# A selective-scan and mixture-of-experts kernel: a new lead-in, and the steady order of the rounds from the first round on

## What is computed

```python
xr = x @ W_in;  xi, res = jnp.split(xr, 2, axis=-1)
u = silu(conv4(xi) + conv_b)
dbc = u @ W_x                       # 8 columns for delta, 16 for B, 16 for C
delta = softplus(dbc[..., :8] @ W_dt + b_dt)
h = exp(delta * A) * h + delta * B * u        # a scan over time, 16 states
y = (sum_n h * C + u * D) * silu(res)
x = x + y @ W_out
scores = norm(x) @ gate_w.T;  cw = softmax of the two best, else 0
x = x + sum_e cw[e] * (silu(norm(x) @ w1[e].T) @ w2[e].T)
```

## Time and profile before

| | us |
|---|---|
| median of 3 runs | 1105.02 |
| lowest and highest | 1104.96, 1106.01 |
| profiled execution, its own time | 1103.15 |
| span of its trace, first to last instruction | 1101.2 |

### The profile page before, as it was taken

How to read it: one execution, slowest core, us unless ns; L and a number is a source line. 1 busy time by engine, 2 the same in 40 slices (tenths; PEclk the granted TensorE clock), 3 DMA queues, 4 the chain that set the end, 5 groups by cost and what they waited for, 6 DMA issues and landing times.

```text
span 1101.2 us, 18699 instructions
## 1 busy us (share of the span) xinstructions
PE 1037.8 (94%) x6152; PEld 759.1 (69%) x6152; DVE 1012.7 (92%) x1038; ACT 908.2 (82%) x1382; POOL 960.5 (87%) x892
## 2 busy tenths in 40 slices
PE   7558679999999999999999999999999999989997
PEld 4336457777777777767777777777777776767775
DVE  2799999999999999999999999999999999999721
ACT  4967578988999899899989999899989989875533
POOL 3388698998999999999999999999999999799834
PEclk9798889999999999999999999999999999989999
DMA  5321313104031311303131220403130120320000
GB/s 152 157 86 49 116 58 116 59 28 155 2 126 58 126 59 68 115 0 138 44 125 57 91 91 7 172 2 125 57 135 39 68 105 0 136 87 10 11 10 10
DMA packets 39760, 84.03 MB, mean 76 GB/s; under 512 B 5744, under 2 KB 30624, under 8 KB 31392
## 3 DMA queue, kind: packets, MB, share of 16 engines
q1 hardware_dynamic: 36848, 83.05, 21.0%
q10 hardware_dynamic: 2864, 0.38, 0.2%
HBM read 78.70 MB, written 4.72 MB: 76 GB/s over the span
## 4 chain that ended last, share of the span: by engine, by line
PE 84%; DVE 6%; ACT 4%; issue 3%; POOL 1%; DMA 0%; POOLq 0%; ACTq 0%; DVEq 0%
PE work L1384 19%; PE work L1374 18%; PE y_ps L1326 17%; PE work L1246 9%; PE rows L1305 4%; DVE h L984 4%; PE work L1265 3%; PE work L1347 3%; PE work L1230 2%; PE rows L1384 2%; PE work L1256 2%; PE rows L1374 1%; DVE rows L974 1%; PE work L1293 1%; ACT dA L742 1%
## 5 line engine op out<-in xcount | busy, mean ns | idle before, releaser
L471 POOL TENSOR_TENSOR h<-h,c_rows 128x1024 f32<-128x1024 f32 x256 | 600.4, 2367 | 75.1 <-DVE h L984 75.0
L984 DVE TENSOR_TENSOR_SCAN h<-dA,rows 128x1024 f32<-128x1024 f32 x256 | 579.4, 2276 | 1.9 <-ACT dA L742 0.7
L742 ACT ACTIVATE dA<-delta,a_neg 128x510 f32<-128x510 f32 x512 | 325.4, 708 | 1.7 <-POOL delta L455 0.5
L974 DVE TENSOR_TENSOR rows<-du,rows 128x1024 f32<-128x1024 f32 x256 | 307.1, 1213 | 3.7 <-PE rows L1305 3.6
L1326 PEld LDWEIGHTS y_ps<-ident,h 128*128 128x128 f32 x2048 | 242.6, 145 | 52.2 <-issue 36.3
L1326 PE MATMUL y_ps<-ident,h 128*128 128x128 f32 x2048 | 267.5, 278 | 2.6 <-POOL h L471 2.6
L1384 PEld LDWEIGHTS work<-w,hid 128*128 128x128 f32 x1856 | 223.2, 193 | 36.5 <-ACT hid L776 20.8
L1374 PE MATMUL work<-x2T,w 128*128 128x512 f32 x474 | 238.3, 597 | 0.3
L1384 PE MATMUL work<-w,hid 128*128 128x128 f32 x1856 | 229.0, 277 | 3.5 <-ACT hid L776 3.2
L776 ACT ACTIVATE hid<-work 128x512 f32<-128x512 f32 x237 | 139.2, 596 | 58.7 <-PE work L1374 56.8
L511 POOL TENSOR_TENSOR x<-x,weighted 128x512 f32<-128x512 f32 x128 | 163.4, 1277 | 23.4 <-DVE weighted L1053 23.0
(11 more groups left out here) (118 smaller groups left out, 953.9 us busy)
## 6 DMA issues: line engine op xcount, KB each, us to landing
c_rows<-c_dram SPq DMA_DIRECT2D x64, 1024.0 KB, 5.2
x_in<-in_x SPq DMA_DIRECT2D x16, 256.0 KB, 2.9
x_again<-in_x SPq DMA_DIRECT2D x16, 256.0 KB, 3.2
out<-x SPq DMA_DIRECT2D x16, 256.0 KB, 2.6
w<-in_w1T SPq DMA_DIRECT2D x1, 1024.0 KB, 6.3
w<-in_w2T SPq DMA_DIRECT2D x1, 1024.0 KB, 8.4
h<-in_conv_w SPq DMA_DIRECT2D x1, 512.0 KB, 4.9
c_dram<-bcd SPq DMA_DIRECT2D x16, 32.0 KB, 1.6
```

The lines of the kernel that those rows point to most:

```text
L471: nc.gpsimd.tensor_tensor(at, at, c_rows[:, n, :].unsqueeze(1).broadcast_to([P, H, T]), ALU.mult).then_inc(c_used, 1)
L742: last = nc.scalar.activation(two_seqs(dA[:, n % RING, half, :])[:, :, 1:], two_seqs(delta[:, half, :])[:, :, 1:], ACT.Exp, scale=a_neg[:, ...
L974: nc.vector.tensor_tensor(rows[:, n % 2], du[:, j.odd], rows[:, n % 2, H - 1, :].unsqueeze(1).broadcast_to([P, H, T]), ALU.mult).then_inc( ...
L984: nc.vector.tensor_tensor_scan(h[:, n % RING].rearrange("p h t -> p (h t)"), dA[:, n % RING].rearrange("p h t -> p (h t)"), rows[:, n % 2] ...
```

## The change

The lead-in is written anew in all engines, and round 0 no longer has its gate, skip and first `row_b` in it: these run where `round_` has them, in round 1.

- W_x comes in one DMA to a spare part of `h`; GpSimd copies it to its places in seven instructions. W_dt comes once more, as float32 rows `w_dt_first`, before x of round 1, which now precedes the six loads of W_dt.
- ScalarE loads Silu's table at the start by a small activation.
- VectorE makes mean and variance with `bn_aggr`; GpSimd only does the power; VectorE makes the shift. Half of the normalized x is made by ScalarE and half by VectorE. Half of `w_conv` is made by VectorE and half by GpSimd.
- WARM is 27 and not 40.
- The projection to delta, B and C starts with its first half when the first half of u is there. One ScalarE copy takes all 112 rows from the bank, and the first delta is projected from it in float32, beside the split into parts, not behind it.
- Abs and Exp run by halves on ScalarE, Relu is on VectorE, and Ln, delta and du run by halves.

```diff
+LEAD_BCD = 2
+LEAD_DT = (4, 5)
-        LOADS = 14
+        LOADS = 4
+        COPIES = 3 * H + 1
-        WARM = 40
+        WARM = 27
...
+        def weigh_taps(engine, half):
+            at = slice(half * P, (half + 1) * P)
+            engine.tensor_tensor(w_conv[:, :, at], w_in[:, at].unsqueeze(1).broadcast_to([P, TAPS, P]),
+                                 taps_rows.rearrange("p (d k) -> p k d", k=TAPS)[:, :, at],
+                                 ALU.mult).then_inc(w_conv_ready, 1)
 SyncE
                 load(skip_w[:, :], D)
+                sp.wait_ge(w_dt_first_clear, 1)
+                sp.dma_start(w_dt_first[DT_ROWS[0]:DT_ROWS[0] + RANK, :], W_dt).then_inc(w_dt_first_loaded, 16)
+                fetch_x(Round(1))
                 sp.wait_ge(dt_rows_clear, 1)
...
-                fetch_x(Round(1))
 GpSimd
             pool.wait_ge(constants_ready, CONSTANTS)
+            pool.wait_ge(w_x_loaded, 16)
+            for half in range(H):
+                part_rows = w_bc[:, half, 0:3 * SPLIT].rearrange("p (a r) -> p a r", a=3)
+                for row, src in ((0, w_x[:, half, RANK:RANK + NS]),) + tuple(
+                        (row, w_x[:, half, 0:RANK]) for row in DT_ROWS):
...
+            nc.gpsimd.tensor_copy(w_bc[:, :, C_ROW:ROWS], w_x[:, :, RANK + NS:]).then_inc(w_bc_ready, 1)
+            pool.wait_ge(variance_ready[0], 1)
+            nc.gpsimd.tensor_tensor(rstd[:, 0, :], variance[:, 0, :], power[:, 0:TB],
+                                    ALU.pow).then_inc(variance_ready[0], 1)
+            pool.wait_ge(taps_loaded, 16 * TAP_LOADS)
+            weigh_taps(nc.gpsimd, 1)
 ScalarE
             def gate_silu(j, half):
-                if not there(j) or j.led():
+                if not there(j):
             def skip(j):
-                if not there(j) or j.led():
+                if not there(j):
             def lead_in():
-                pre_norm(lead)
+                act.wait_ge(constants_ready, CONSTANTS)
+                nc.scalar.activation(warm[:, :], one[:, :], ACT.Silu).then_inc(tables_warm, 1)
+                act.wait_ge(rstd_ready[0], 1)
+                for b in range(TB // 2):
+                    last = nc.scalar.activation(xn[:, 0, b, :], x_in[:, 0, b, :], ACT.Identity,
...
                 for half in range(H):
                     conv_silu(lead, half)
-                skip(lead)
-                high(lead)
-                copy_bcd(lead)
-                middle(lead)
-                gate_silu(lead, 0)
-                low(lead)
-                gate_silu(lead, 1)
                 exp_tables()
-                for half in range(H):
-                    soft_parts(lead, half)
-                soft_exponential(lead)
-                soft_log(lead)
+                act.wait_ge(bcd_projected, 1)
+                nc.scalar.activation(bcd[0:ROWS, :], bcd_bank(lead)[0:ROWS], ACT.Copy).then_inc(bcd_ready, 1)
                 (a_neg, as before)
+                for half in range(H):
+                    act.wait_ge(dt_projected, half + 1)
+                    nc.scalar.activation(soft[:, half, :], bank(LEAD_DT[half]), ACT.Abs,
...
+                    nc.scalar.activation(soft[:, half, :], soft[:, half, :], ACT.Exp,
...
+                middle(lead)
+                for half in range(H):
+                    act.wait_ge((lead_exp, soft_exp)[half], 1)
+                    nc.scalar.activation(soft[:, half, :], soft[:, half, :], ACT.Ln,
...
+                low(lead)
 TensorE
             def project_gate(j, half, *uses):
-                if not there(j) or j.led():
+                if not there(j):
             def row_b(j, n):
-                if not there(j) or (n < 2 and j.led()):
+                if not there(j):
             def lead_in():
...
+                for half in range(H):
+                    pe.wait_ge(u_ready, half + 1)
+                    last = nc.tensor.matmul(bcd_bank(lead), w_bc[:, half, :], u[:, 0, half, :], start=(half == 0),
+                                            stop=(half == H - 1))
+                pe.wait_ge(bcd_ready, 1)
+                for half in range(H):
+                    nc.tensor.matmul(bank(LEAD_DT[half]), w_dt_first[:, half * P:(half + 1) * P], bcd[0:SPLIT, :],
+                                     start=True, stop=True).then_inc(dt_projected, 1)
                 take_high(lead)
-                project_gate(lead, 1)
                 take_middle(lead)
-                for half in range(H):
-                    delta_rank(lead, half, *([use_dt(lead, 0)] if half and DT[0] == DT[1] else []))
                 pe.wait_ge(select_ready, 1)
-                row_b(lead, 0)
-                row_b(lead, 1)
                 pe.wait_ge(dt_read, H)
```

More of the change, by code:

```diff
@@ L105, in wait, with run @@
             eng.wait_ge(sem, value)
-    def run(eng, body, stages, stop):
-        loop_first = stages + 2
+    def run(eng, body, first, stages, stop):
+        loop_first = max(first, stages + 2)
         pairs = (min(rounds, stop) - loop_first) // 2
-        for i in range(loop_first):
+        for i in range(first, loop_first):
             body(Round(i))
@@ L291, in place, with bcd_bank @@
             return k
+        def bcd_bank(j):
+            return bank(LEAD_BCD if j.lead else BCD)
         def two_seqs(ap):
@@ L424, in inverse_deviation @@
             def inverse_deviation(j, k):
-                if not there(j):
+                if not there(j) or (k == 0 and j.led()):
                     return
@@ L607, in _ @@
         def _(act):
-            def load(dst, src):
-                act.dma_start(dst, src).then_inc(weights_loaded, 16)
             act.dma_start(w_in[:, :], W_in).then_inc(taps_loaded, 16)
[L612 to L619, removed]
+            act.dma_start(w_x[:, :, :], W_x.rearrange("(h p) n -> p h n", p=P)).then_inc(w_x_loaded, 16)
             tables = ["none"]
@@ L667, in gate_silu @@
                 wait(act, gated, j.count(1, -1))
-                nc.scalar.activation(gate[:, j.odd, half, :], bank(LEAD_GATE[half] if j.lead else GATE[half]),
-                                     ACT.Silu).then_inc(gate_ready, 1)
+                nc.scalar.activation(gate[:, j.odd, half, :], bank(GATE[half]), ACT.Silu).then_inc(gate_ready, 1)
             def copy_bcd(j):
@@ L1123, in split_dt_weights, with first_norm @@
                 dve.wait_ge(dt_weights_ready, 2)
+            def first_norm():
+                pre_stats(r[0])
+                dve.wait_ge(stats_ready[0], 1)
+                for b in range(TB):
+                    last = nc.vector.bn_aggr(mean_variance[:, b, :], stats[:, 0, b, :])
+                last.then_inc(moments_ready[0], 3)
+                dve.wait_ge(moments_ready[0], 3)
+                nc.vector.tensor_scalar(variance[:, 0, :], mean_variance[:, :, 1], EPS, None,
+                                        ALU.add).then_inc(variance_ready[0], 1)
+                dve.wait_ge(taps_loaded, 16 * TAP_LOADS)
+                weigh_taps(nc.vector, 0)
+                dve.wait_ge(variance_ready[0], 2)
+                nc.vector.scalar_tensor_tensor(shift[:, 0, :], mean_variance[:, :, 0], -1.0, rstd[:, 0, :], ALU.mult,
+                                               ALU.mult).then_inc(rstd_ready[0], 1)
+                dve.wait_ge(rstd_ready[0], 1)
+                for b in range(TB // 2, TB):
+                    last = nc.vector.tensor_scalar(xn[:, 0, b, :], x_in[:, 0, b, :], rstd[:, 0, b:b + 1],
+                                                   shift[:, 0, b:b + 1], ALU.mult, ALU.add)
+                last.then_inc(lead_norm, 1)
@@ L1255, in project_gate @@
                 at = (H + half) * P
-                nc.tensor.matmul(two_seqs(bank(LEAD_GATE[half] if j.lead else GATE[half])), w_in[:, at:at + P], xnT[:, :, PAD:],
+                nc.tensor.matmul(two_seqs(bank(GATE[half])), w_in[:, at:at + P], xnT[:, :, PAD:],
                                  start=True, stop=True).then_inc(gate_projected, 1)
@@ L1264, in project_bcd @@
                 for half in range(H):
-                    last = nc.tensor.matmul(work[:, BCD, :], w_bc[:, half, :], u[:, j.odd, half, :],
+                    last = nc.tensor.matmul(bcd_bank(j), w_bc[:, half, :], u[:, j.odd, half, :],
                                             start=(half == 0), stop=(half == H - 1))
```

102 lines of the change are left out of this document (67 added, 35 removed).

## The result

The changed kernel takes 1109.56 us (median of 6 runs, 1109.33 to 1109.77) against 1105.37 us before (6 runs): a ratio of 1.0036 with a 95% interval of 1.0023 to 1.0049.

A forecast was written before the change was run, and what follows sets the result against it. The prediction took VectorE's start on its scans as the early bound, passed on to rounds where TensorE is full. Scan 2 at 45.15 and not 46.76 us gave 1105.02 less 1.6, 1103.4 us; range 1101.4 to 1105.8.

The forecast's parts named there:

- scan 2 is handed on: VectorE's scan of state 2 in round 0, at 46.76 us before: any shift is passed on one for one.
- (d): Rival: the gain is real but lost later, where TensorE takes over as the bound; 1105 us, chance 0.05.
- The sum at scan 2: Lead-in and round 1 terms added up to the start of round 0's scan 2: 45.15 us, 1.6 us earlier.
- Part 1: Lead-in until round 0's convolution starts: at 11.95 us, 1.0 us earlier, bounds 0.2 to 2.2 us.
- rival (b): TensorE's pause before the first convolution lowers its clock, costing 1.5 to 1.9 us; 1104.8 to 1105.3 us, chance 0.17.
- Part 2: Round 0's convolution to the end of ScalarE's low part: at 27.4 us; delta and du some 6 us earlier.
- Part 3: ScalarE's round 1 queue ahead of decay 0 takes the 6 us back: scan 0 at 38.2 us, 0.3 us later.
- Part 4: TensorE's round 1 convolution ends earlier, row 2 ready at 43.5 us; scan 2 hangs on VectorE alone, gaining 1.6 us.
- Rival (c): Slower: ScalarE's queue between low and decay 0 delays scan 0 by 2 to 4 us; 1105.5 to 1107.5 us, chance 0.08.

The follow-up runs named there:

- e2: The changed kernel with GpSimd's half of w_conv made by VectorE, right behind VectorE's own half: 1109.06 us.
- e4: The changed kernel with round 0's gate projections moved to the lead-in, its gate silus and skip term behind round 1's convolution silus: 1102.19 us, 0.9966 of before.
- e5: The changed kernel with nine tiny unused ScalarE activations more in the lead-in, ahead of the loop: 1108.07 us.
- e6: The changed kernel with e4's edits, w_conv's second half on VectorE behind its normalized x, 40 warm-up transposes and eleven tiny activations: 1098.38 us, 0.9942 of before.
- e1: The changed kernel with 44 warm-up transposes and not 27: 1109.44 us, 1.0029 of before.
- e3: The changed kernel with w_conv wholly on VectorE and 36 warm-up transposes and not 27: 1107.90 us.

## Why the prediction was wrong

**In short.** Three steps of the sum failed: the longer pause behind the shorter WARM, costed at nothing, took 2.8 us in the convolution of round 0; GpSimd's half of w_conv, counted as hidden, took 1.3 us in VectorE's shift; and the gate's second projection, costed at the full clock, took 1.0 us more. A stall in the loop, which no term of the sum covers, added 1.5 us.

**What bounds the kernel, and that scan 2 is handed on: right in the main.** From scan 2 of round 0 to that of round 4 the difference moves by 0.2 us at most in the changed kernel, e2, e4, e5 and e6, over differences of -5.0 to +4.2 us. It isn't one for one everywhere: in e1 and e3, and in the second trace of the kernel before, another 0.5 to 0.7 us was lost between scan 2 of round 0 and that of round 2. So the rival that a gain is lost later (d) is out for the large gains of e4 and e6, but it describes e1, where 1.0 us became 0.2.

**The sum at scan 2 was off by 5.8 us** (45.15 forecast, 50.95 measured), and its terms measure:

| term | forecast | measured |
|---|---|---|
| end of the power | 9.4 | 9.46 |
| shift | 0.2 | 1.47 |
| start of the convolution of round 0 | 11.95 | 13.56 |
| that convolution | 7.1 | 9.92 |
| end of that convolution to the end of low | 8.3 | 8.5 |
| low to scan 0 | 10.8 | 12.0 |
| scan 0 to scan 2 | 6.95 | 6.9 |

The power's end came out right by luck: W_x let the first copy begin at 6.82 and not 6.4 us and the seven copies took 0.1 us more, while the first-use cost, of which half was counted, didn't come.

Part 1 failed at the shift. I counted GpSimd's half of w_conv as hidden because nothing waits for it before 11.6 us, and didn't ask who runs beside it: VectorE's shift does, on the path, and took 1.3 us more. In e2 and e6, where GpSimd's multiply isn't beside it, the shift takes 0.16 us. The handovers between the steps are the other 0.3 us by which the convolution started later than forecast. The Trainium skill says of the shift's neighbour, in "GPSIMD Engine Reference", section Specifications: that GpSimd's interfaces to SBUF are shared with VectorE, and that they contend, among other cases, when VectorE's instruction has two inputs in SBUF. The trace agrees: the shift has two such inputs (1.47 for 0.16 us), and VectorE's multiply for w_conv, with two as well, made GpSimd's six copies 2.42 us long for 1.49. The steady rounds give no warning of it: a scan takes 2.29 us with GpSimd idle (37.92 us) and with a GpSimd multiply from 40.35 to 42.72 us beside it (41.36 us); but there one of the scan's inputs, rows, lies in PSUM.

Part 1 failed also at WARM, costed at nothing with a rival (b) of 0.17. The late shift lengthened the pause from the forecast 1.7 us to 2.86 us, and the clock fell. That this pause decides it rests on the nine traces: in the three with a pause of at most 1.81 us the convolution took 7.11 us, in the six with 2.35 us or more it took 8.57 to 10.03. The rival had the mechanism but priced it at 1.5 to 1.9 us, from the convolution of round 1, and its time ended at 1105.3 us; it was 2.8 us here. That the two faults feed each other (the later the shift, the longer the pause) is what I had not seen. The end of the 27 transposes was forecast well (9.2 us, and 9.17 measured), but again with luck: they began 0.23 us later than in the kernel before, where the first two dozen took 5.2 us and not 5.5.

Part 2 was right to 0.2 us, and the new softplus does what it should: from the end of the convolution to the end of the last Ln it is 8.1 us, where it was 12.6. VectorE's delta and du ended at 33.9 and not near 29 us, by the 4.4 us that the convolution ended late and its halves of 0.69 us for 0.62, but nothing waited for them.

Part 3 had the mechanism (what was gained is spent in ScalarE's queue ahead of decay 0) and its direction; the mis-sized term is the gate's second projection, taken at the full clock (1.05 us, and 2.05 measured, at a granted clock of 0.50). With its handovers it kept ScalarE waiting 2.23 us, 1.2 more than forecast, which is the whole difference between 10.8 and 12.0. e4 shows how dear the part is: moving the gate and the skip term out of it gives 5.0 us at scan 2. Part 4 was right: scan 2 hung on VectorE alone, and row 2 was there at 49.2 us, 0.5 us before it was asked for. The Trainium skill, in "ScalarE: Activation LUTs", section What ACT_TABLE_LOAD costs, adds a drain of the pipeline to each table load of about 1.28 us; the trace doesn't agree, since the next activation starts 1.30 and 1.29 us after the load began (32.04 and 33.34, 41.33 and 42.62 us), and the loads begin 0.02 us after the activation in front of them ended.

**Beyond the sum**, the loop's stalls cost 1.5 us, for a cause that no row of the kernel before could show, though a page with 43 loads beside one with 23 does. And the baseline: I took the distance of 1.87 us between profiled execution and median as a constant. It isn't one: it was 0.1 us in the changed kernel. A second trace of the kernel before, at 1106.62 us, loses most of its time by the clock in rounds 0 and 1. But the clock isn't all of it: among the 53 executions of the kernel before that ran beside and as experiments, 17 have a mean granted clock of 0.978, and six of these took 1103.0 to 1103.3 us, eleven 1104.8 to 1105.4. No trace shows an execution of the second group, which is where the first median lies, so what sets these 1.8 us stays open. Between the two profiled executions the loss is 6.3 us (4.2 at scan 2, 1.5 in the loop, 0.5 in the end); between the medians it is 4.2, since the usual execution of before is 2 us slower than the one I read. That 4.2 is also the difference at scan 2 is a coincidence of these terms. Rival (c) had the side of the result and the place of 1.2 us of it, ScalarE's queue between low and decay 0, but gave as instances table loads, which took 1.28 us as forecast, and slow copies, of which only the first was slow (0.76 us).

## What to carry to other kernels

When a small instruction is on the path, look at what the other engine does in those microseconds, not only at who waits for it: work moved to a free engine is hidden only if it doesn't slow the instructions of the path that run beside it. When a start-up path is rearranged, count each pause of TensorE on it, since a late operand is paid again as a slower clock behind it. And if every pass of a loop slips by the same amount after an edit elsewhere, look at the instruction loads before looking for a wait.

## What the runs showed of the hardware

- The same number of transposes ends at different times from one execution to the next (40 of them in 7.46 us, and in 5.99), because their pace doubles, from 0.22 to 0.11 us each, at a different moment: at 8.9 us in one trace of the kernel before and at 5.9 us in the other. Pauses of 0.71, 1.12 and 1.81 us before the first transpose of x kept the full clock for the convolution (7.11 us each time); pauses of 2.35, 2.51, 2.52, 2.83, 2.86 and 3.34 us did not (8.57, 8.71, 10.03, 9.92, 9.92 and 9.26 us). A longer pause didn't always cost more.
- A VectorE instruction of 128x4 elements with two inputs in SBUF took 1.47 us for 0.16, until a GpSimd multiply beside it ended; of GpSimd copies that take 0.2 us otherwise, one took 0.76 us and one 1.08 us, and each ended within 0.1 us of a VectorE multiply with two inputs in SBUF.
- A loop of ScalarE ran with no instruction load at all in one place of the program, and with five loads of 8 KB and a pause of about 1 us in each pass in a place nine instructions earlier. In e4, eleven instructions of ScalarE fewer than in e5, it had the five loads and pauses of 0.3 to 0.6 us.
